# A gated two-layer block on one core: the passage from the first attention into the feed-forward reordered (a bank-freeing addition ahead of the third sum of x, copies of transposed x behind the copy of a half, later chunks later)

## The reference, cut to what matters

```python
x = x + tanh(g_xattn[0]) * L0_xattn(_layernorm(x), ctx, ctx, W, b)      # attention to 154 keys
x = x + tanh(g_ffn[0])   * L0_ffn(_layernorm(x), Wg, Wu, Wd)            # the feed-forward
x = x + tanh(g_xattn[1]) * L1_xattn(_layernorm(x), ...)                 # 8 heads
x = x + tanh(g_ffn[1])   * L1_ffn(_layernorm(x), ...)                   # top-1 routed experts

def L0_ffn(x, Wg, Wu, Wd):          # for each of 8 dense experts
    h = silu(x @ wg) * (x @ wu)     # 256 -> 1024
    acc = acc + h @ wd              # 1024 -> 256
```

## Time and the profile before

| | |
|---|---|
| time, median of 3 executions | 1256.4 us (1256.3, 1256.4, 1260.84) |
| the profiled execution's own time | 1260.54 us |
| its span | 1258.8 us |
| mean granted clock of TensorE over the span | 0.995 |
| TensorE busy | 98% of the span |
| VectorE, GpSimd, ScalarE busy | 84%, 70%, 58% |

### The profile page before, as it was taken

One profiled execution on the slowest core, in us unless ns is written; L12 is line 12 of the kernel. 1 busy time (PEld: TensorE's weight loads), 2 busy tenths in 40 slices (PEclk: granted clock), 3 DMA queues, 4 the chain that ended last, 5 costly groups with the idle time before them and its releaser, 6 DMA issues.

```text
span 1258.8 us, 18431 instructions
## 1 busy us (share of the span) xinstructions
PE 1232.6 (98%) x6152; PEld 995.4 (79%) x6152; DVE 1054.3 (84%) x1775; ACT 729.2 (58%) x1509; POOL 880.5 (70%) x833
## 2 busy tenths in 40 slices
PE   7999999999999999999999999999999999999998
PEld 5778888888888888888888888888888887787775
DVE  5887889898899999999999999888999974667546
ACT  2455566656666666666666666666566545545543
POOL 3735688888887888888877888888888626443435
PEclk9999999999999999999999999999999999999999
DMA  4020200000110000000000000000100330000131
GB/s 137 26 92 1 94 26 26 26 26 26 41 36 26 26 26 26 26 26 26 26 26 26 26 26 26 26 26 31 42 29 1 117 118 1 18 26 10 35 98 63
DMA packets 42366, 48.28 MB, mean 38 GB/s; under 512 B 4239, under 2 KB 40143, under 8 KB 42015
## 3 DMA queue, kind: packets, MB, share of 16 engines
q1 hardware_dynamic: 38720, 43.07, 10.4%
q0 software_dynamic: 1440, 3.41, 0.8%
q10 hardware_dynamic: 2111, 0.63, 0.2%
HBM read 37.36 MB, written 10.29 MB: 38 GB/s over the span
## 4 chain that ended last, share of the span: by engine, by line
PE 91%; DVE 4%; ACT 3%; issue 1%; DMA 0%; POOLq 0%; ACTq 0%; POOL 0%; DVEq 0%
PE bank L1307 25%; PE bank L1308 25%; PE bank L1309 25%; ACT PC L1050 2%; PE bank L1545 2%; PE bank L1554 1%; PE bank L1269 1%; PE bank L1707 1%; PE bank L1724 1%; PE bank L1251 1%; DVE nmC L2101 1%; PE bank L1529 1%; PE bank L1213 1%; PE bank L1657 1%; PE bank L1479 1%
## 5 line engine op out<-in xcount | busy, mean ns | idle before, releaser
L1307 PE MATMUL bank<-xop_hi,w_hi 128*128 128x512 f32 x896 | 351.9, 393 | 1.7 <-ACT half_g L948 1.2
L1308 PE MATMUL bank<-xop_lo,w_hi 128*128 128x512 f32 x896 | 352.4, 393 | 0.0
L1309 PE MATMUL bank<-xop_hi,w_lo 128*128 128x512 f32 x896 | 351.4, 392 | 0.0
L1958 DVE TENSOR_TENSOR hid_lo<-hid,hid_hi 128x512 fp32r<-128x512 f32 x228 | 220.2, 979 | 14.1 <-ACT hid_hi L972 9.8
L1307 PEld LDWEIGHTS bank<-xop_hi,w_hi 128*128 128x128 f32 x896 | 168.9, 188 | 42.4 <-ACT half_g L948 1.5
L1308 PEld LDWEIGHTS bank<-xop_lo,w_hi 128*128 128x128 f32 x896 | 168.6, 188 | 38.2
L1309 PEld LDWEIGHTS bank<-xop_hi,w_lo 128*128 128x128 f32 x896 | 168.6, 188 | 37.7
L972 ACT CAST hid_hi<-hid 128x512 fp32r<-128x512 f32 x228 | 140.8, 622 | 57.9 <-DVE hid L1950 57.9
L956 ACT ACTIVATE s<-bank 128x512 f32<-128x512 f32 x128 | 78.3, 612 | 102.5 <-PE bank L1309 102.5
L1307 PE MATMUL bank<-hid_hi,wd_hi 128*128 128x512 f32 x344 | 136.2, 396 | 0.6 <-DVE hid_lo L1958 0.6
L1308 PE MATMUL bank<-hid_lo,wd_hi 128*128 128x512 f32 x344 | 136.2, 396 | 0.0
(11 more groups left out here) (273 smaller groups left out, 2615.1 us busy)
## 6 DMA issues: line engine op xcount, KB each, us to landing
raw_gu<-in_L_ffn_Wg_dram SPq DMA_DIRECT2D x32, 256.0 KB, 2.7
raw_gu<-in_L_ffn_Wu_dram SPq DMA_DIRECT2D x32, 256.0 KB, 3.1
raw_d<-in_L_ffn_Wd_dram SPq DMA_DIRECT2D x32, 256.0 KB, 3.7
slots<-empty_row SPq DMA_DIRECT2D x1, 2080.0 KB, 11.1
xr<-slots SPq DMA_DIRECT2D x8, 260.0 KB, 4.5
x_res<-in_x_dram SPq DMA_DIRECT2D x4, 512.0 KB, 5.3
x_mid<-x_res SPq DMA_DIRECT2D x1, 2048.0 KB, 9.2
x_res<-x_mid SPq DMA_DIRECT2D x4, 512.0 KB, 5.4
```

The lines of the kernel that those rows point to most:

```text
L1307: mm(ps, w, a, start=start, stop=False, skip_group_check=True)
L1308: mm(ps, w, a_low, start=False, stop=False, skip_group_check=True)
L1309: return mm(ps, w_low, a, start=False, stop=True, skip_group_check=True)
L1958: nc.vector.tensor_tensor(out=hid_lo[n % 2][h][:], in0=hid[h][:], in1=hid_hi[n % 2][h][:].bitcast(F32), op=ALU.subtract).then_inc(lo_ready ...
```

## The change

Five edits of order. No arithmetic is added or taken away.

1. Attention, chunk 3: on TensorE the transposes of chunk 3's probabilities stand between the two halves of chunk 2's product with the values instead of behind both; on ScalarE their copy out stands ahead of the first two roundings of x instead of behind them.
2. VectorE: sum T2 goes ahead of the second half of chunk 2's addition (which frees bank 7), and so that addition now stands ahead of sum T3; the variances of chunk 2 go behind the sums T3 and T4 and the first two remainders, and the norm of chunk 2 two remainders later; the variances of chunk 3 go into group 0, behind `sum_12` of `g`, and the norm of chunk 3 between the two hidden blocks.
3. TensorE, group 0: the transposes of chunk 2 go from ahead of product 7 of `g` to behind product 3 of `u`; those of chunk 3 go from group 0 to group 1, behind product 1 of `u`.
4. ScalarE: the copies of chunk 2 go from behind the forks to behind `keep_u2` of `u`; those of chunk 3 from the end of group 0 to behind the forks of group 1.
5. ScalarE: the roundings of the hidden blocks 22 and 12 of group 0 go from the end of group 0 to behind the first fork of group 1.

```diff
@@ ScalarE, end of the attention
             x_raw_out(1)
+            a_pT_out(NC - 1)
             x_hi_first(0)
-            a_pT_out(NC - 1)
@@ ScalarE, the groups
                 fork(n, "g")
+                if n == 1:
+                    hi_part(0, "22")
+                    hi_part(0, "12")
                 hi_part(n - 1, "11")
                 fork(n, "u")
-                if n == 0:
-                    x_raw_out(2)
+                if n == 1:
+                    x_raw_out(3)
...
                 keep_u2(n, "u")
+                if n == 0:
+                    x_raw_out(2)
...
-                if n == 0:
-                    x_raw_out(3)
                 if n == 1:
                     x_hi_rest(1)
-                hi_part(n, "22")
-                hi_part(n, "12")
+                if n > 0:
+                    hi_part(n, "22")
+                    hi_part(n, "12")
@@ TensorE, attention
-                a_p_transposes(u)
+                if u < NC - 1:
+                    a_p_transposes(u)
...
-                a_attend(u)
+                if u == NC - 2:
+                    a_attend(u, range(2))
+                    a_p_transposes(NC - 1)
+                    a_attend(u, range(2, CT))
+                else:
+                    a_attend(u)
@@ TensorE, the groups
                 product1(n, "u")
+                if n == 1:
+                    x2_transposes(NC - 1)
...
-                if n == 0:
-                    x2_transposes(NC - 2)
                 product7(n, "g")
...
                 product3(n, "u")
+                if n == 0:
+                    x2_transposes(NC - 2)
                 product7(n, "u")
...
-                if n == 0:
-                    x2_transposes(NC - 1)
@@ VectorE, end of the attention
             x_first_sum(nc.vector, dve, 0)
+            dve.wait_ge(x_raw_ready, 4)
+            dve.wait_ge(x_sum_ready[0], 1)
+            x_sum(nc.vector, 0, X_T2, X_22, X_T1)
             a_add_half(2, 1)
-            ln2_variances(2)
-            x_other_sums(nc.vector, dve, 0)
+            x_sum(nc.vector, 0, X_T3, X_22, X_T3)
+            dve.wait_ge(x_sum_ready[0], 2)
+            x_sum(nc.vector, 0, X_T4, X_21, X_T2)
             for i in range(2):
                 x_lo_out(nc.vector, dve, 0, i)
-            ln2_normed(2)
+            ln2_variances(2)
             for i in range(2, 4):
                 x_lo_out(nc.vector, dve, 0, i)
+            ln2_normed(2)
+            for i in range(4, 6):
+                x_lo_out(nc.vector, dve, 0, i)
             a_add(3)
-            for i in range(4, 7):
-                x_lo_out(nc.vector, dve, 0, i)
-            ln2_variances(3)
+            x_lo_out(nc.vector, dve, 0, 6)
@@ VectorE, group 0
                 sum_22(n, "g")
-                if n == 0:
-                    ln2_normed(3)
                 sum_12(n, "g")
                 if n == 0:
+                    ln2_variances(3)
                     sum_22(n, "u")
...
                 hid_sum(n, "22", half22, sum22)
+                if n == 0:
+                    ln2_normed(3)
                 hid_sum(n, "12", half12, sum12)
```

More of the change, by code:

```diff
@@ L1261, in a_p_transposes, with a_attend @@
                     ins.then_inc(a_pT_ps, 1)
-            def a_attend(u):
+            def a_attend(u, of=range(CT)):
                 pe.wait_ge(a_pT, 2 * u + 2)
-                for j in range(CT):
+                for j in of:
                     if u > 0 and j % 2 == 0:
```

## The result

The change is slower, by less than a fifth of a per cent: 1258.74 us (median of 12, 1257.41 to 1261.42) against 1256.85 us for the kernel before (12, 1256.24 to 1260.84), a ratio of 1.0018 with a 95% interval of [1.001, 1.0025]. I had forecast 1255.6 us, a little faster; it came out a little slower, and the interval leaves out 1. The profiled execution took 1260.8 us (span 1259.0), almost what the one before took (1260.54, span 1258.8).

The account below looks back on a forecast made before the run. TensorE, busy 98% of the span, bounds the kernel, and VectorE the changed passage. Of 3.3 us gained, 2.45 were low clock, assumed absent from the 1256.4 us median, leaving 0.85 and a forecast of 1255.6 us (range 1253.6 to 1259.6).

Parts of the forecast that it names:

- Steps 1 to 3: Attention's end, group 0 and group 1: new order carried to the first product of group 2 at 91.3 us, not 94.64.
- first product: First product of the feed-forward, after the attention's end: forecast to start at 62.5 us instead of 64.97.
- wait ahead of 7g: TensorE in group 0, ahead of product 7 of g: forecast a wait of 0.2 us instead of 1.22.
- wait ahead of 4u: TensorE ahead of product 4 of u: forecast a new wait of 2.1 us for VectorE's `sum_22` of u.
- wait ahead of the first down product: TensorE in group 1: forecast a wait of 0.4 us for ScalarE's copies of chunk 3, product starting at 80.9.
- The sum: Start of group 2: 3.3 us earlier, 2.45 from the low clock and 0.85 from order; old order 92.2 at full clock.
- The clock falls at the new wait: Rival: TensorE's clock falls near 75 us, behind the wait ahead of 4u; 1256.7 to 1258.4 us; chance 0.25.
- The first low stretch stays: Rival: TensorE's clock still low from 61.6 to 68.4 us, perhaps from the attention's small matmuls; median 1257.1 us; chance 0.12.
- VectorE is faster than charged: Rival: VectorE faster or waits smaller than carried; without the 2.1 us wait, 1253.5 us; chance 0.08.
- Less than that works: Rival: VectorE meets GpSimd's sums, a pair 1 remainder is late, or second low stretch comes oftener; 1257.5 to 1259.5 us; chance 0.1.

Follow-up runs that it names:

- b_again: The kernel before, unedited, run again; 1257.52 us, ratio 1.0002 to before.
- copy3_first: The change with ScalarE's rounding of hidden block 11 of group 0 moved behind the copies of chunk 3; 1257.29 us, ratio 0.9996 to before.
- a_no_p1: The change with edit 1 (the attention's end) undone; 1257.91 us, ratio 1.0004 to before.
- chunk2_later: The kernel before with only chunk 2's transposes and copies moved to where the change puts them; 1256.42 us, ratio 0.9998 to before.
- attention_end: The change with edits 3, 4, 5 and the group-0 part of edit 2 undone; 1261.24 us, ratio 1.0035 to before.
- before_gpsimd: The kernel before with chunk 2's transposes and copies later and pair 0's last three remainders on GpSimd; 1261.5 us, ratio 1.0033 to before.
- gpsimd_rest_2: The change with three remainders on GpSimd, chunk 3's addition before chunk 2's norm, block 11's rounding behind chunk 3's copies; 1255.62 us, ratio 0.9996 to before.
- a_again: The change, unedited, run again; 1257.96 us, ratio 1.0009 to before.

## Why the prediction failed, point by point

**Steps 1 to 3, the carry of the new order, held.** Before's profile has the transposes of chunk 1 at 52.84 us, the one after at 52.30, so 0.54 is taken off my times.

| | forecast, less 0.54 | measured |
|---|---|---|
| first product | 62.0 | 61.84 |
| wait ahead of 7g | 0.2 | 0.54 |
| wait ahead of 4u, released by `sum_22` of u | 2.1 | 1.60 |
| wait ahead of the first down product | 0.4 | 0.45 |
| first down product | 80.4 | 80.64 |
| first product of group 2 | 90.8 | 91.17 |

What 7g waited more, 4u waited less. That VectorE bounds the passage held too.

**The step that failed is "The sum": the same carry for the order before.** There I wrote 92.2 us for the start of group 2 at full clock, 91.7 less the 0.52 us by which b_again's transposes of chunk 1 are earlier, with waits of 1.1, 0.2, 1.4 and 1.2 us, "an earlier TensorE waits more". Measured it is 90.64, 1.0 us earlier. In b_again the 1.4 is 1.22, and the 0.2 and the 1.2 do not exist. I took over the 2.38 us of two hidden blocks, which VectorE needed beside GpSimd's four sums in one execution, and put a TensorE without the low clock in front of them. The timelines of VectorE and GpSimd there, in the kernel before:

```profile
79.20 1.80 POOL L436 TENSOR_TENSOR xop_raw<-xop_raw 128x512 f32<-128x512 f32 x1 [6.23 <-ACT xop_raw L881]
79.77 1.78 DVE L1950 TENSOR_TENSOR hid<-half_u,half_g 128x512 f32<-128x512 f32 x1
```

and in b_again:

```profile
76.26 2.44 POOL L436 TENSOR_TENSOR xop_raw<-xop_raw 128x512 f32<-128x512 f32 x1 [3.80 <-ACT xop_raw L881]
76.26 0.68 DVE L1950 TENSOR_TENSOR hid<-half_u,half_g 128x512 f32<-128x512 f32 x1
76.86 0.68 DVE L1950 TENSOR_TENSOR hid<-half_u,half_g 128x512 f32<-128x512 f32 x1
```

Both times GpSimd's first sum and VectorE's first hidden block start within 0.03 us of each other. Before, the sum came in between the two blocks, and the second took 1.78 us; in b_again both blocks came first, at 0.6 us each, and the sum took 2.44 us in place of 1.80. The row that I carried was one outcome of two.

In place of −0.85 us the order is worth +0.55 at the start of group 2 (38.87 us from the transposes of chunk 1 against 38.32), as at Q, and +0.42 at the first down product. Of the 1.4 us between forecast and measurement 1.0 is the old order carried too late and 0.4 the new one carried too early. The low clock of 6.8 us, which I put at 2.45 us, cost more: before and b_again differ by 31.40 − 27.92 = 3.48 us at the first down product, and by 2.92 already at product 4u (25.80 against 22.88), ahead of the longer hidden blocks. I had measured the gain against a passage that the low clock had lengthened, and split it by a model of the old order for which no row at full clock stood.

**What the change trades.** It takes off 1.07 + 1.22 us of waits and puts on 0.54 + 1.60 + 0.45 (with the small ones, 2.50 us in b_again against 2.96 after). Two of the three new ones are for VectorE, whose amount of work no edit changes; the third is a queue on ScalarE that copy3_first shows was avoidable.

**From 1.9 to 0.4 us.** The medians of the first comparison differ by 1.9 us, the passage by 0.4 to 0.55. By mean clock, medians of the change are 1257.37 us at 1.000 (6), 1257.91 at 0.998 (5) and 1258.74 at 0.997 (4), those of before 1256.43 (40), 1257.03 (28) and 1257.73 (17): 0.9 to 1.0 us at each. So about 1 us of the 1.9 goes with the changed kernel at equal mean clock. The traces show 0.4 to 0.55 of it as the order of the passage; the other half I did not locate. The rest is the mix: 8 of 24 executions of the change have a mean clock of 0.995 or less, 19 of the 105 of before whose clock is on record. Whether the change makes low stretches likelier or these counts are chance stays open.

**The rivals.** *The clock falls at the new wait*: it ended on the right side, for the wrong reason. No profile of the change shows a low clock near 75 us, after waits of 1.60 and 1.63 us, and those of a_no_p1 (1.51) and copy3_first (1.66) show none either. At this wait the traces decide against the rule of the Trainium skill (TensorE: Matmul & The Clock Gate, section on psum-queue depth-cycling) that the rival cites. For the low stretches in the last attention they leave it open: TensorE has gaps of 0.70 and 0.46 us there ahead of the fall at 1050.6 us, and the same two gaps in chunk2_later, where no fall follows. *The first low stretch stays*: not in either profile of the change; the same order has it in one execution and not in another, as before and b_again show. *VectorE is faster than charged*: no; it was charged right to 0.1 us. *Less than that works*: the time (1258.7) lies in its range, and its clause on the second low stretch coming oftener describes the profile after, but its other mechanisms are not seen.

**The median.** I took the median executions for ones without any low stretch. For the kernel before that is 0.6 us off (1256.43 at 1.000 against 1256.99 over all 105). And the upper end of my range doesn't follow from its own terms: 1258.4 with a low stretch of 6.8 us and 1.7 for a further one make 1260.1, not 1259.6.

## What to carry to other kernels

When an expected gain is the difference of two carries, carry the old order too and compare it with a trace of it under the same conditions: the new order came out right to half a microsecond, and the difference had the wrong sign. Don't carry a duration that was read beside another busy engine into another schedule without a bound for it. Where one engine's queue sets the end of a passage, count that engine's work ahead of the point: reordering others mostly moves the waits, and here handing 1.9 us of work to an engine with room, with one addition moved, gained 1.7 us, where five edits of order lost 0.4. Before giving work to another engine's queue, look up who waits for what stands behind it.

## What the runs showed of the hardware

**The clock.** The same kernel, with the same 1.07 us wait and the same rows around it, had the clock at 0.50 for 6.8 us in one execution and at 1.00 in the other. Between executions of the kernel before the time ran from 1256.4 us at a mean clock of 1.000 (40 executions) to 1260.3 at 0.995 (18): 3.9 us, more than the change or the best order moved it. A comparison of such kernels should be made at equal mean clock.

Two much longer waits went with a fall each time they were profiled. In attention_end the clock fell 1.8 us after a wait of 3.17 us, in before_gpsimd 2.5 us into one of 3.83 us. None of these two kernels' 14 executions has a mean clock above 0.997, where 68 of 105 of the kernel before have. After waits of 1.5 to 1.81 us no profile shows a fall in this passage, while one followed the 1.07 us wait in the profile of the kernel before and none in b_again. Two kernels are few, and the experiments were not made to separate this from chance.

**The start.** Where the clock first rose at 12.9 to 13.0 us, the transposes of chunk 1 started 45.2 to 45.3 us behind the first matmul, and 46.5 where it rose at 15.9: 1.2 us of an execution that no edit caused. The mean clock doesn't show it: gpsimd_rest_2 with the early rise and a_again with the late one both have 1.000. Two executions at equal mean clock can so still differ by this much.

**VectorE beside GpSimd.** Where both engines have two inputs in SBUF, the rows add up as if they took turns: before, GpSimd's sum of 1.80 us holds the rest of VectorE's first block (0.57 to 0.6) and its own 1.2, and VectorE's second block of 1.78 holds that 1.2 and its own 0.6; in b_again GpSimd's 2.44 holds two blocks of 0.6 and its own 1.2. The Trainium skill (SBUF — State Buffer, section on two separate sides) says that they take a shared port pair in turn; the traces agree. They add that with the two starts within 0.03 us of each other VectorE paid the 1.2 us in one execution and GpSimd in the other.
